# A state-space layer on one core: where the transposed blocks are kept, when they are loaded back, and what stands ahead of the multiply by dt

## The chip, the cores and the metric

The kernel runs on one core of a Trainium2 chip. The metric is the device time of one execution in microseconds (us): 1695.08 us as the median of three runs (1694.08 to 1696.36).

The engines are TensorE (PE in the profile; its weight loads are PEld), VectorE (DVE), ScalarE (ACT), GpSimd (POOL) and SyncE (SP). Here SyncE issues all of the transfers. Each engine works through its own list of instructions in order, and semaphores are what holds one list back for another.

## The reference

Input is `x` of 2 x 512 tokens of width 512. The layer is a Mamba-2 block with a residual, then a dense layer with summed low-rank experts and another residual:

```
proj  = layernorm(x) @ in_proj_w.T             # gate 8192 | x 8192, B 1024, C 1024 | dt 128
hBC   = silu(causal_conv(x, B, C; 4 taps))
dt    = clip(softplus(dt + dt_bias), 0, 100);  A = -exp(A_log)
xch   = hs * dt                                # 128 heads of 64, chunks of 128 tokens
Y     = (C B^T * exp(segsum(dt*A))) @ xch      # inside a chunk
      + C @ (states carried over the chunks)   # states = B^T @ (decay * xch)
      + hs * D
g     = Y * silu(gate);  g = g * rsqrt(mean over each of 8 groups of g^2 + 1e-5)
x     = x + (g * norm_w) @ out_proj_w.T
x     = x + layernorm(x) @ W.T + b + sum_e probs_e (layernorm(x) @ A_e.T) @ B_e.T
```

Everything is fp32. The large products are made of three: weight and input are each split into a high part that TensorE's fp32r form holds and the rest (`w_high`, `w_low`), and high x high, high x low and low x high are added.

## The kernel before

The work is cut into 64 units. A unit k is 128 of the 8192 inner channels, that is two heads, over all 1024 tokens; eight units (j = 0 to 7) are one group g, which shares B and C. Each engine has a hand-written function `body(g, last)`, which goes through the eight j and issues for unit k what is due, and for unit k+1 (`ahead`) what can be done early. Nothing but the order of these calls and the semaphores sets the schedule.

TensorE's body for unit k: the last two output products of the unit before (`later_outs`, c = 2 and 3), the projection of the x channels of unit k+1 into `x_bank` (24 matmuls of 512 columns), `states(k)`, which needs `xdecay`, then `diagonal(k)`, the gate projection of unit k+1 into `g_bank` (24 more), `carry(k)`, and the output products c = 0 and 1. Bodies 4 and 5 of a group also project B and C of the next group, and bodies 6, 7 and 0 have smaller products.

The path of unit k+1 from its convolution to `xdecay` is this. ScalarE's `tap0` writes tap 0 from `x_bank` into `hs`. VectorE's `tap` adds taps 1 to 3 (L1234), ScalarE applies silu (L1079). VectorE's `turn_blocks` (L1317) transposes each 32 x 32 block of `hs`; SyncE's `store_blocks` (L714) stores the result to `blocks_dram` in DRAM (512 KB), and after the store has landed `load_quads` (L721) brings it back with four transfers into `quads` in another arrangement, so that tokens are on the partitions. VectorE's `to_heads` (L1332) multiplies `quads` by dt into `xdt`, in two instructions; GpSimd's `decayed` (L1526) multiplies `xdt` by the decay into `xdecay`, one instruction for each of the two batches b. Only then can TensorE start `states(k+1)` (L823).

Before the change, `turn_blocks(k+1)` writes its result over the `hs` buffer of unit k, so it comes after `skip(k)` (L1296, the last reader of that buffer), and ScalarE's `tap0` waits for the store of the blocks that lie where it writes. SyncE issues, between the store and `load_quads`, the four transfers of `load_grown` (L707), which wait for VectorE's `add_carry` (L1303). On VectorE `to_heads(k)` stands behind the two scores multiplications (L1266) and behind `add_outs` for c = 2 and 3 (L1355, or the copy at L1352 in two of the eight units), which wait for TensorE's `later_outs`. In bodies 5 and 6 it stands behind the three taps of B or C (L1243) as well.

Behind `to_heads(k)` VectorE has `y_low_part` (L1250), in body 1 also the sum of squares and the reciprocal, in bodies 1, 2 and 3 `normed_out` (L1359, two, three and three instructions), and then the taps of unit k+1.

## Time and profile before

| | |
|---|---|
| median of three runs | 1695.08 us |
| the profiled execution: its own time | 1687.36 us |
| its span, first to last instruction | 1685.6 us |
| PE busy | 1570.0 us (93%) |
| DVE busy | 1376.5 us (82%) |
| ACT busy | 1149.9 us (68%) |
| POOL busy | 758.2 us (45%) |
| mean granted TensorE clock | 0.984 |

The span is the time between the first and the last instruction of the profiled execution; its own time is 1.8 us more. Busy times can overlap between engines. The first `states` starts at 69.6 us and the last at 1621.4 us, so the 64 units take some 1552 us of the span; what is before is the first layernorm and the tables, what is after is the last group's norm and the dense layer. In the profile's rows "[1.98 <-POOL xdecay L1526]" means that the engine stood idle for 1.98 us before this instruction and that the instruction named released it.

### The profile page before, as it was taken

What the parts mean: (1) busy time and instruction counts of PE and PEld (TensorE: products, weight loads), DVE (VectorE), ACT (ScalarE), POOL (GpSimd) and SP (SyncE); (2) the same over time, 40 slices, a digit from 0 to 9 for tenths busy, and PEclk for the clock granted to TensorE, in tenths of its full rate; (3) what the DMA queues carried; (4) which work ended last, traced back from release to release, by engine and by line L of the source; (5) the groups of instructions that cost most, each with busy time, mean ns of one, the idle gap of its engine ahead of it and who ended that gap; (6) DMA issues with size and microseconds to landing.
All of it is one profiled execution on the core that took longest, in us unless ns stands there. A gap on an engine that the chain in (4) does not pass through costs nothing.

```text
span 1685.6 us, 26384 instructions
## 1 busy us (share of the span) xinstructions
PE 1570.0 (93%) x9072; PEld 1311.4 (78%) x9072; DVE 1376.5 (82%) x2047; ACT 1149.9 (68%) x2020; POOL 758.2 (45%) x535
## 2 busy tenths in 40 slices
PE   7879999899998999999999999989999899999988
PEld 5667888787887788778887788777788778877767
DVE  7677878887888878887788888788878987888777
ACT  5966667666786677666577667666677767776643
POOL 2244444454445444445345535445444544545440
PEclk9999999999999999999999999999999999999989
DMA  4554434443443344344444344434344334343321
GB/s 150 201 159 129 156 124 134 154 143 108 157 150 127 119 150 149 127 136 129 129 160 138 124 146 136 128 132 156 105 146 160 130 117 158 137 142 126 132 66 51
DMA packets 132278, 228.43 MB, mean 136 GB/s; under 512 B 28080, under 2 KB 76720, under 8 KB 131888
## 3 DMA queue, kind: packets, MB, share of 16 engines
q1 hardware_dynamic: 132144, 226.74, 41.0%
q8 instruction: 73, 1.20, 0.3%
q14 instruction: 61, 0.50, 0.1%
HBM read 187.87 MB, written 38.80 MB: 134 GB/s over the span
## 4 chain that ended last, share of the span: by engine, by line
issue 55%; POOL 36%; PE 7%; ACT 1%; DVE 0%; DMA 0%; SPq 0%; POOLq 0%; ACTq 0%; DVEq 0%
POOL w_low L1505 9%; POOL xdecay L1526 8%; POOL square_sum L1513 8%; POOL y L1519 6%; POOL out_low L1544 5%; PE head_bank L823 0%; PE d_bank L834 0%; DMA alog<-a_log 0%; PE head_bank L298 0%; PE g_bank L814 0%; PE g_bank L884 0%; PE d_bank L903 0%; PE g_bank L816 0%; PE head_bank L903 0%; PE d_bank L904 0%
## 5 line engine op out<-in xcount | busy, mean ns | idle before, releaser
L1526 POOL TENSOR_TENSOR xdecay<-xdt,tables 128x384 f32<-128x384 f32 x128 | 165.7, 1314 | 478.5 <-DVE xdt L1332 468.4
L1054 ACT ACTIVATE scores<-scores,tables 128x128 f32<-128x128 f32 x1024 | 312.0, 389 | 0.0
L1519 POOL TENSOR_TENSOR y<-y,gate 128x512 f32<-128x512 f32 x128 | 179.5, 1423 | 272.0 <-DVE y L1303 272.0
L1234 DVE SCALAR_TENSOR_TENSOR hs<-x_bank,cols,hs 128x1022 f32<-128x1022 f32 x189 | 241.6, 1278 | 29.9 <-ACT hs L1067 25.3
L814 PE MATMUL g_bank<-x_high,w_high 128*128 128x512 f32 x624 | 251.0, 402 | 0.0
L816 PE MATMUL g_bank<-x_high,w_low 128*128 128x512 f32 x624 | 243.4, 390 | 0.0
L815 PE MATMUL g_bank<-x_low,w_high 128*128 128x512 f32 x624 | 243.4, 390 | 0.0
L1505 POOL TENSOR_TENSOR w_low<-raw,w_high 128x512 fp32r<-128x512 f32 x139 | 184.9, 1330 | 102.6 <-ACT w_high L1044 102.5
L1067 ACT ACTIVATE hs<-x_bank,cols 128x1024 f32<-128x1024 f32 x63 | 75.7, 1201 | 215.8 <-PE x_bank L816 186.0
L823 PE MATMUL head_bank<-xdecay,b_tok 128*128 128x128 f32 x768 | 120.4, 308 | 90.8 <-POOL xdecay L1526 83.8
L814 PE MATMUL x_bank<-x_high,w_high 128*128 128x512 f32 x504 | 196.4, 390 | 1.8 <-issue 1.8
L823 PEld LDWEIGHTS head_bank<-xdecay,b_tok 128*128 128x128 f32 x768 | 104.3, 207 | 119.0 <-POOL xdecay L1526 106.9
L815 PE MATMUL x_bank<-x_low,w_high 128*128 128x512 f32 x504 | 196.1, 389 | 0.0
L816 PE MATMUL x_bank<-x_high,w_low 128*128 128x512 f32 x504 | 196.1, 389 | 0.0
L1266 DVE TENSOR_TENSOR scores<-scores,bc 128x1024 f32<-128x1024 f32 x128 | 174.6, 1375 | 1.4 <-ACT scores L1059 1.4
L814 PEld LDWEIGHTS g_bank<-x_high,w_high 128*128 128x128 f32 x624 | 117.0, 188 | 33.5 <-issue 11.0
L1513 POOL TENSOR_TENSOR square_sum<-square_sum,gate 128x1024 f32<-128x1024 f32 x55 | 137.4, 2499 | 0.0
L816 PEld LDWEIGHTS g_bank<-x_high,w_low 128*128 128x128 f32 x624 | 117.1, 188 | 25.4
L815 PEld LDWEIGHTS g_bank<-x_low,w_high 128*128 128x128 f32 x624 | 117.3, 188 | 22.7 <-issue 0.2
L834 PE MATMUL d_bank<-scores,xdt 128*64 128x128 f32 x2048 | 134.8, 288 | 0.0
L1355 DVE TENSOR_TENSOR acc<-d_bank,acc 128x512 f32<-128x512 f32 x94 | 64.6, 687 | 83.0 <-PE d_bank L873 83.0
L1059 ACT ACTIVATE scores<-scores 128x1024 f32<-128x1024 f32 x128 | 128.6, 1053 | 0.7
(213 smaller groups left out, 3457.6 us busy)
## 6 DMA issues: line engine op xcount, KB each, us to landing
scores<-sums_dram SPq DMA_DIRECT2D x128, 512.0 KB, 4.9
raw<-w_in SPq DMA_DIRECT2D x144, 256.0 KB, 2.7
blocks_dram<-hs SPq DMA_DIRECT2D x63, 512.0 KB, 2.6
quads<-blocks_dram SPq DMA_DIRECT2D x252, 128.0 KB, 3.0
grown_rows<-grown_dram SPq DMA_DIRECT2D x256, 96.0 KB, 2.8
out_raw<-w_out SPq DMA_DIRECT2D x64, 256.0 KB, 3.3
mixed<-x SPq DMA_DIRECT2D x8, 256.0 KB, 4.6
out<-mixed SPq DMA_DIRECT2D x8, 256.0 KB, 2.0
```

The source lines that it names most:

```text
L814: pe.matmul(to, w_high[:, slot, k], x_high[:, b, k], start=(k == 0), stop=False)
L815: pe.matmul(to, w_high[:, slot, k], x_low[:, b, k], start=False, stop=False)
L816: mm = pe.matmul(to, w_low[:, slot, k], x_high[:, b, k], start=False, stop=(k == KT - 1))
L823: mm = pe.matmul(head_bank[b][:, c * P:(c + 1) * P], b_tok[:, b, c], xdecay[:, b, c].rearrange("p r d -> p (r d)"), start=True, stop=True)
L834: mm = pe.matmul(d_bank[r * HEAD_DIM:(r + 1) * HEAD_DIM, b, c * P:(c + 1) * P], xdt[:, b, c, r], scores[:, s, b, r, c], start=True, stop=True)
L1054: op = s.activation(at, at, ACT.Relu, bias=col[:, r, c:c + 1], scale=-1.0)
L1234: v.scalar_tensor_tensor(out=hs[:, q % 2, :, i:], in0=x_bank[:, :, 0:SEQ - i], scalar=cols[:, q, TAPS - 1 - i:TAPS - i], in1=hs[:, q % 2, ...
L1266: v.tensor_tensor(at, at, bc[:, b].rearrange("p c l -> p (c l)").unsqueeze(1) .to_broadcast([P, PAIR, SEQ]), ALU.mult).then_inc(scores_rea ...
L1505: pool.tensor_tensor(w_low[:, slot], raw[:, slot], w_high[:, slot].bitcast(F32), ALU.subtract)\
L1513: pool.tensor_tensor(square_sum[:], square_sum[:], gate[:, q % 2], ALU.add).then_inc(square_added, 1)
L1519: pool.tensor_tensor(y[:, b], y[:, b], gate[:, q % 2, b], ALU.mult).then_inc(y_ready, 1)
L1526: pool.tensor_tensor(xdecay[:, b], xdt[:, b, 0:LATER], col.unsqueeze(3).to_broadcast([P, LATER, PAIR, HEAD_DIM]), ALU.mult)\
```

## The change

It has three parts.

1. `turn_blocks(k+1)` writes into `quads`, the buffer that `load_quads` fills later, and no longer into the `hs` buffer of unit k. It therefore no longer waits for `skip(k)` and is called ahead of it; it waits for `to_heads(k)` (`xdt_ready`), the last reader of `quads`, instead. ScalarE's `tap0` no longer waits for the store. `load_quads` drops its own wait for `xdt_ready`.
2. SyncE issues `load_quads` directly behind `store_blocks`, ahead of the four transfers of `load_grown`.
3. On VectorE, the scores and `to_heads(k)` come ahead of `add_outs` for c = 2 and 3, and in bodies 5 and 6 ahead of the taps of B and C.

```diff
--- before.py
+++ after.py
@@ -672,9 +672,7 @@
         def bank_of(j, c):
             return last_bank[c] if j == UNITS + 1 else out_bank[c]
 
-        def blocks_of(k):
-
-            return hs[:, (k - 1) % 2].rearrange("p b n -> p (b n)")
+        blocks = quads[:].rearrange("p a b c i -> p (a b c i)")
 
         def table_of(kind, b, q):
             return tables[:, b, q // HALF, kind, PAIR * (q % HALF):PAIR * (q % HALF + 1)]
@@ -711,11 +709,10 @@
                 sp.wait_ge(blocks_turned, k)
                 for m in range(QUADS):
                     reached(sp, moved[m], 16 * (k - 1))
-                sp.dma_start(blocks_dram, blocks_of(k)).then_inc(blocks_stored, 16)
+                sp.dma_start(blocks_dram, blocks).then_inc(blocks_stored, 16)
 
             def load_quads(k):
                 sp.wait_ge(blocks_stored, 16 * k)
-                sp.wait_ge(xdt_ready, PAIR * k)
                 by_part = blocks_dram.rearrange("(a j) (m n) -> m j a n", a=QUADS, m=QUADS)
                 for m in range(QUADS):
                     sp.dma_start(quads[m * QUAD:(m + 1) * QUAD].rearrange("p a b c i -> p a (b c i)"), by_part[m])\
@@ -775,9 +772,9 @@
                         load_weight(*at)
                     if ahead:
                         store_blocks(ahead[2])
+                        load_quads(ahead[2])
                         for b in range(BATCH):
                             load_grown(ahead[2], b)
-                        load_quads(ahead[2])
                     for at in then if len(splits) == SPLIT else []:
                         load_weight(*at)
                     if last and j == UNITS - 1:
@@ -1063,7 +1060,6 @@
                     s.wait_ge(cols_in[q // HALF], 16 * (g + 1))
                 s.wait_ge(projected, BATCH * (tile_number(g, place(g, q)) + 1))
                 reached(s, skip_added, k - 1)
-                reached(s, blocks_stored, 16 * (k - 1))
                 s.activation(hs[:, q % 2], x_bank[:], ACT.Identity, scale=cols[:, q, TAPS - 1:TAPS],
                              bias=cols[:, q, TAPS:TAPS + 1]).then_inc(tap0_ready, 1)
 
@@ -1313,8 +1309,8 @@
 
             def turn_blocks(k):
                 v.wait_ge(hs_ready, k + 1)
-                v.wait_ge(skip_added, k)
-                v.transpose(blocks_of(k).rearrange("p (m n i) -> p n m i", m=QUADS, i=QUAD),
+                reached(v, xdt_ready, PAIR * k)
+                v.transpose(blocks.rearrange("p (m n i) -> p n m i", m=QUADS, i=QUAD),
                             hs[:, k % 2].rearrange("p b (c m i) -> p (b c) m i", c=CHUNKS, i=QUAD))\
                  .then_inc(blocks_turned, 1)
 
@@ -1417,20 +1413,16 @@
                     if k == 0:
                         for b in range(BATCH):
                             first_heads(b)
-                    if k > 2:
-                        add_outs(g, j - 1, (2,))
+                    if last or j not in (5, 6):
+                        for b in range(BATCH):
+                            score(g, j, k, b)
+                    if k > 0:
+                        to_heads(g, j, k)
                     if j in (5, 6) and not last:
                         for i in range(1, TAPS):
                             bc_tap(i, 2 * (g + 1) + j - 5, j - 5)
-                    scores_here = last or j not in (5, 6)
-                    if scores_here:
-                        score(g, j, k, 0)
                     if k > 2:
-                        add_outs(g, j - 1, (3,))
-                    if scores_here:
-                        score(g, j, k, 1)
-                    if k > 0:
-                        to_heads(g, j, k)
+                        add_outs(g, j - 1, (2, 3))
                     if j == UNITS - 1 and not last:
                         keep_bc(g + 1, g_bank)
                     if prev and ahead:
@@ -1447,8 +1439,8 @@
                     for b in range(BATCH):
                         carried_state(*now, b)
                     if ahead:
+                        turn_blocks(k + 1)
                         skip(j, k)
-                        turn_blocks(k + 1)
                         for b in range(BATCH):
                             carry_part(k, b)
                         for b in range(BATCH):
```

No instruction is added or removed; what moves is their order. The line numbers of the changed kernel are two to four lower. In its rows, L1313 is `turn_blocks`, L1292 `skip`, L1328 `to_heads`, L1262 the scores.

VectorE in a middle unit of a group, from the end of body k to the first part of body k+1, before:

```order
L1296 SCALAR_TENSOR_TENSOR y<-hs,cols,d_bank 128x1024
L1317 STREAM_TRANSPOSE hs<-hs 128x8x4x32
L1291 TENSOR_TENSOR grown_rows<-head_bank,grown_rows 128x384 x2
L1303 TENSOR_TENSOR y<-y,grown_rows 128x384 x2
L1355 TENSOR_TENSOR acc<-x_bank,acc 128x512 x2
L1355 TENSOR_TENSOR acc<-d_bank,acc 128x512
L1266 TENSOR_TENSOR scores<-scores,bc 128x1024
L1355 TENSOR_TENSOR acc<-d_bank,acc 128x512
L1266 TENSOR_TENSOR scores<-scores,bc 128x1024
L1332 TENSOR_TENSOR xdt<-quads,tables 128x8x64 x2
L1250 SCALAR_TENSOR_TENSOR y_low<-y,cols,y_high 128x1024
```

and with the change:

```order
L1313 STREAM_TRANSPOSE quads<-hs 128x8x4x32
L1292 SCALAR_TENSOR_TENSOR y<-hs,cols,d_bank 128x1024
L1287 TENSOR_TENSOR grown_rows<-head_bank,grown_rows 128x384 x2
L1299 TENSOR_TENSOR y<-y,grown_rows 128x384 x2
L1351 TENSOR_TENSOR acc<-x_bank,acc 128x512 x2
L1262 TENSOR_TENSOR scores<-scores,bc 128x1024 x2
L1328 TENSOR_TENSOR xdt<-quads,tables 128x8x64 x2
L1351 TENSOR_TENSOR acc<-d_bank,acc 128x512 x2
L1246 SCALAR_TENSOR_TENSOR y_low<-y,cols,y_high 128x1024
```

The transpose now stands ahead of `skip`, and both additions from `d_bank` stand behind `xdt`.

VectorE at the start of body 5, where the taps of B are, before:

```order
L1355 TENSOR_TENSOR acc<-x_bank,acc 128x512 x2
L1266 TENSOR_TENSOR scores<-scores,bc 128x1024 x2
L1355 TENSOR_TENSOR acc<-d_bank,acc 128x512
L1243 SCALAR_TENSOR_TENSOR bc_conv<-g_bank,tap_bc,bc_conv 128x2x511
L1243 SCALAR_TENSOR_TENSOR bc_conv<-g_bank,tap_bc,bc_conv 128x2x510
L1243 SCALAR_TENSOR_TENSOR bc_conv<-g_bank,tap_bc,bc_conv 128x2x509
L1355 TENSOR_TENSOR acc<-d_bank,acc 128x512
L1332 TENSOR_TENSOR xdt<-quads,tables 128x8x64 x2
L1250 SCALAR_TENSOR_TENSOR y_low<-y,cols,y_high 128x1024
```

and with the change:

```order
L1351 TENSOR_TENSOR acc<-x_bank,acc 128x512 x2
L1262 TENSOR_TENSOR scores<-scores,bc 128x1024 x2
L1328 TENSOR_TENSOR xdt<-quads,tables 128x8x64 x2
L1239 SCALAR_TENSOR_TENSOR bc_conv<-g_bank,tap_bc,bc_conv 128x2x511
L1239 SCALAR_TENSOR_TENSOR bc_conv<-g_bank,tap_bc,bc_conv 128x2x510
L1239 SCALAR_TENSOR_TENSOR bc_conv<-g_bank,tap_bc,bc_conv 128x2x509
L1351 TENSOR_TENSOR acc<-d_bank,acc 128x512 x2
L1246 SCALAR_TENSOR_TENSOR y_low<-y,cols,y_high 128x1024
```

Here `xdt` moves ahead of five instructions, three of which are the taps of B.

SyncE's queue in a middle unit, before:

```order
L700 DMA scores<-sums_dram 128x1024 x2
L692 DMA raw<-w_in 128x512
L714 DMA blocks_dram<-hs 128x1024
L707 DMA grown_rows<-grown_dram 64x384 x4
L721 DMA quads<-blocks_dram 32x4x256 x4
L696 DMA out_raw<-w_out 128x512
```

and with the change:

```order
L698 DMA scores<-sums_dram 128x1024 x2
L690 DMA raw<-w_in 128x512
L712 DMA blocks_dram<-quads 128x1024
L718 DMA quads<-blocks_dram 32x4x256 x4
L705 DMA grown_rows<-grown_dram 64x384 x4
L694 DMA out_raw<-w_out 128x512
```

The four loads of `quads` and the four of `grown_rows` have changed places.

## Rows read from the trace of the kernel before

**Rows 1.** Page part 1: busy us, share of the span, instructions

```profile
PE 1570.0 (93%) x9072; PEld 1311.4 (78%) x9072; DVE 1376.5 (82%) x2047; ACT 1149.9 (68%) x2020; POOL 758.2 (45%) x535
```

**Rows 2.** Waits over the whole span: total us, times, longest us

```profile
PE head_bank L823 <- POOL xdecay L1526: 83.8, 57, 5.1
...
DVE xdt L1332 <- DMA quads<-blocks_dram: 49.8, 32, 3.1
...
PE head_bank L823 <- issue: 6.9, 7, 2.0
```

**Rows 3.** Timeline of TensorE, units 8 to 11: start us, us, instruction, [idle before]

```profile
267.23 1.69 PE L823 MATMUL head_bank<-xdecay,b_tok 128*128 128x128 f32 x12 [0.82 <-issue]
...
289.59 1.73 PE L823 MATMUL head_bank<-xdecay,b_tok 128*128 128x128 f32 x12
291.26 1.97 PE L834 MATMUL d_bank<-scores,xdt 128*64 128x128 f32 x32
...
313.10 0.94 PE L823 MATMUL head_bank<-xdecay,b_tok 128*128 128x128 f32 x6 [1.98 <-POOL xdecay L1526]
...
337.70 0.94 PE L823 MATMUL head_bank<-xdecay,b_tok 128*128 128x128 f32 x6 [2.58 <-POOL xdecay L1526]
338.94 1.11 PE L823 MATMUL head_bank<-xdecay,b_tok 128*128 128x128 f32 x6 [0.31 <-POOL xdecay L1526]
339.99 3.41 PE L834 MATMUL d_bank<-scores,xdt 128*64 128x128 f32 x32
```

**Rows 4.** Timeline of VectorE, body of unit 10, then xdt of unit 11

```profile
316.45 3.90 DVE L1234 SCALAR_TENSOR_TENSOR hs<-x_bank,cols,hs 128x1022 f32<-128x1022 f32 x3
...
322.69 1.27 DVE L1296 SCALAR_TENSOR_TENSOR y<-hs,cols,d_bank 128x1024 f32<-128x1024 f32 x1
324.07 1.25 DVE L1317 STREAM_TRANSPOSE hs<-hs 128x1024 f32<-128x1024 f32 x1
...
334.46 1.29 DVE L1332 TENSOR_TENSOR xdt<-quads,tables 128x512 f32<-128x512 f32 x2 [2.08 <-DMA quads<-blocks_dram]
335.67 1.28 DVE L1250 SCALAR_TENSOR_TENSOR y_low<-y,cols,y_high 128x1024 fp32r<-128x1024 f32 x1
```

**Rows 5.** Timeline of SyncE's DMA issues in the same stretch

```profile
325.35 0.32 SPq L714 DMA_DIRECT2D blocks_dram<-hs  x1
...
329.19 1.95 SPq L721 DMA_DIRECT2D quads<-blocks_dram  x4
```

**Rows 6.** DMA issues: KB each, median us to landing

```profile
blocks_dram<-hs SPq DMA_DIRECT2D x63, 512.0 KB, 2.6
quads<-blocks_dram SPq DMA_DIRECT2D x252, 128.0 KB, 3.0
```

**Rows 7.** Timeline of GpSimd in units 11 and 31

```profile
335.83 3.06 POOL L1526 TENSOR_TENSOR xdecay<-xdt,tables 128x384 f32<-128x384 f32 x2 [6.27 <-DVE xdt L1332]
...
838.89 1.64 POOL L1526 TENSOR_TENSOR xdecay<-xdt,tables 128x384 f32<-128x384 f32 x2 [7.01 <-DVE xdt L1332]
```

**Rows 8.** Line 1359 on VectorE: ns least/median/most, first and last start

```profile
L1359 DVE SCALAR_TENSOR_TENSOR mixed<-acc,g_rstd,mixed x64: 741/1324/1761, 290.6 to 1671.5; 128x512 f32<-128x512 f32 x64
```

**Rows 9.** Windows: busy us by engine, then PEclk; first and last dip

```profile
93.40:117.70 24.30, 19.52 (x108) 15.59 (x108) 17.16 (x26) 15.80 (x28) 10.05 (x8) 0.93 0.56 179
...
1506.40:1531.00 24.60, 23.20 (x128) 19.31 (x128) 21.88 (x32) 15.46 (x29) 12.88 (x10) 0.93 0.38 134
```

**Rows 10.** Timeline of VectorE, SyncE and TensorE, body of unit 12, then unit 13

```profile
376.19 3.36 DVE L1266 TENSOR_TENSOR scores<-scores,bc 128x1024 f32<-128x1024 f32 x2
382.38 0.69 DVE L1355 TENSOR_TENSOR acc<-d_bank,acc 128x512 f32<-128x512 f32 x1 [2.83 <-PE d_bank L873]
...
387.41 1.29 DVE L1332 TENSOR_TENSOR xdt<-quads,tables 128x512 f32<-128x512 f32 x2
...
374.58 0.32 SPq L714 DMA_DIRECT2D blocks_dram<-hs  x1
...
390.64 1.62 PE L823 MATMUL head_bank<-xdecay,b_tok 128*128 128x128 f32 x11 [1.50 <-POOL xdecay L1526]
```

## The prediction, made before the changed kernel ran

> **What bounds the kernel now.** I read the page's first part, then the waits, then the timeline of each engine over some middle units, then windows for the clock. TensorE is busy for 93% of the span [rows 1], so the question is what ends its idle time. The waits answer it: at the first matmul of `states` (L823) it stood idle for 83.8 us over 57 times because `xdecay` was not there, and 6.9 us more at the same line are put down to issue [rows 2]. That is 90.7 us, most of what TensorE is idle at all (1685.6 - 1570.0 = 115.6 us). Wherever the wait is absent the unit simply takes TensorE's own work: unit 9 comes 22.36 us after unit 8 with no idle time before it, while unit 10 takes 23.51 us of which 1.98 is idle, hence 21.5 us of work, and unit 11 takes 24.60 us with 2.58 idle before it [rows 3].
>
> The idle time costs a second time. In unit 11, behind the 2.58 us, the second six matmuls of `states` and `diagonal` take 1.11 and 3.41 us; in the others they take 0.94 (the first six at 337.70) and 1.97 [rows 3]. That is 1.6 us more, and the windows show why: the granted clock of such a unit is 0.93 of full, that is, one stretch at 1.2 instead of 2.4 GHz right after the idle time. There are eleven such stretches in the main loop, the first and the last in [rows 9]; each comes at a unit that waited about 2 us or more.
>
> So the length of the main loop hangs on when `xdecay` of the next unit is ready. For unit 11 the path is, by start times: taps 316.45, `skip` 322.69, transpose 324.07 [rows 4], store 325.35, then four `grown_rows` issues, the `quads` issues from 329.19 [rows 5], `xdt` 334.46 after VectorE had stood idle 2.08 us for the last of them [rows 4], `states` 337.70 [rows 3]. In bodies 5 and 6 the queue on VectorE is the obstacle, not the transfer: it waits 2.83 us for TensorE's output product, does one addition and the taps of B, and gets to `xdt` at 387.41, though the store had been issued at 374.58 [rows 10].
>
> **The transpose ahead of `skip`.** It stands 324.07 - 322.69 = 1.38 us earlier, and so does the store. What is late next in its place: `skip`, by 1.25 us. Its readers are `carry_part` and `add_carry`, which wait for TensorE's `carry` as well, and that comes behind all 24 matmuls of the gate projection. I cost it at nothing; without that cover 1.25 us would go onto `y_sum` and so onto GpSimd's multiply by the gate, not onto the path to `xdecay`. The transpose costs what it does now, 1.25 us: source and shape are the same, and the wait for `xdt_ready` is for an instruction a whole body earlier on the same engine.
>
> **The loads right behind the store.** Today 329.19 - 325.35 = 3.84 us lie between the store and the first load [rows 5]. The store's landing takes a median of 2.6 us [rows 6] after an issue of 0.32; with the semaphore I take 3.15 us. Gain 0.7 us. Bounds: 0 (the landing is what ended it) and 0.9. SyncE now stands in the wait for the landing with `load_grown` behind it; those loads go out 1 to 2 us later than now, but are read only in the next unit's `carry_part`, behind the next taps, states and transpose. From the first load to `xdt` it takes 334.46 - 329.19 = 5.27 us, unchanged. So `xdt` of unit 11 can start at 322.69 + 1.25 + 0.05 + 3.15 + 5.27 = 332.4, which is 2.1 us earlier, if VectorE is there: the scores ended at 334.46 - 2.08 = 332.38 with two additions among them, and those (0.6 us apart, 0.69 each [rows 10]) are now behind. It is.
>
> **Additions behind `xdt`.** Today `y_low` (L1250) follows `xdt` directly [rows 4] and GpSimd's pair of `xdecay` takes 3.06 us; where in unit 31 the product with the mask from a PSUM bank follows instead, the pair takes 1.64 [rows 7]. Now the additions, which also read a bank, follow everywhere but in bodies 5 and 6 (there it is the taps, which read a bank too). The first half of `xdecay` should be ready about 2.2 us after `xdt` starts, against 3.24 (337.70 - 334.46): 1.0 us more. Bounds 0 and 1.0; I take 1.0, since unit 31 does just this. Likewise `normed_out` (L1359) spans 741 to 1761 ns [rows 8]; its slow cases run beside GpSimd's work. It now comes 1.3 us later, when the shorter pair is over, so I put three of them at about 2.0 us, not 4.
>
> The Trainium skill, SBUF — State Buffer, "Who interferes with whom", says a VectorE instruction with two SBUF inputs and a GpSimd instruction that reads SBUF exclude each other for the whole instruction. The trace agrees (3.06 against 1.64, 741 against 1761). By that rule the change also moves the scores, which have two SBUF inputs, further into GpSimd's multiply by the gate, and this speaks against it; the first rival below carries that case.
>
> So for unit 11: 2.1 + 1.0 = 3.1 us earlier, against 2.58 + 0.31 us of idle time. The wait is gone there. Does it stay gone once TensorE moves faster? The ring that closes from `xdt` to the next `xdt` in units with three `normed_out` is 1.2 (`xdt`) + 1.25 (additions) + 1.8 (`y_low`, part of it behind GpSimd) + 2.0 + 6.24 (taps to transpose, 322.69 - 316.45) + 1.3 + 3.15 + 5.27 = 22.2 us, against TensorE's 21.5. It loses 0.7 us a unit for two units, 1.4, and has 3.1 - 1.98 = 1.1 in hand from unit 10. I leave 0.3 us of idle time in seven groups: 2 us.
>
> **Bodies 5 and 6.** `xdt` can start at 374.58 + 3.15 + 5.27 = 383.0 instead of 387.41, 4.4 us earlier against 1.50 us of idle time (the last row of [rows 10]). VectorE then waits for `quads` (it used to wait for the output product). Queued behind: `xdt` itself 1.2, taps of B 3.9 (by the taps of [rows 4]), additions 1.25, `y_low` 1.2, done at about 390.5. TensorE would end the next projection at 390.64 - 1.50 = 389.1, and `tap0` comes behind that, so the next taps start on time or some tenths late. No idle time is left.
>
> **The sum.** Idle time at L823: 90.7, of which I leave 2 us as above and 3 us in the last unit (it has no projection ahead of `states`; its 5.1 us [rows 2] shrink by 2.1): 85.7 gained. Half-clock stretches: 10 of 11 go, 10 x 1.6 = 16. Together 101.7. Against the profiled execution's own time: 1687.36 - 101.7 = 1585.7. The median of the runs is 7.7 us above that execution (1695.08 - 1687.36); I expect the same of the new one and say **1594 us**, with 1582 to 1608 as its own range.
>
> **Rival 1: VectorE becomes the bound in bodies 1 to 4.** In unit 11 it was idle for only 2.08 of 24.60 us, so its work there is 22.5, above TensorE's 21.5. If `normed_out` stays slow and two scores take 3.36 us as at 376.19 [rows 10] rather than 2.4, the work is 23.5, 2.0 too much in two units of each group, less 1.1 in hand: 2.9 us, and a clock stretch of 1.6 with it, times 7 = 31 us. About 1625. For it: the figures are all in the trace. Against: the cause of slow `normed_out` moves away. Chance 0.18.
>
> **Rival 2: other waits of TensorE appear** that are hidden now (the gate's silu, `out_low`, the convolution), and half of the gain goes: 1695 - 51 = 1644. Against: unit 9 runs with no wait. Chance 0.05. Nothing would change if `xdecay` were in truth held by something else than `xdt`, yet GpSimd stands idle for 6.27 us before the pair of unit 11 [rows 7] and starts it right behind `xdt`: 0.02, at 1695.
>
> **Rival 3: slower.** `to_heads` now stands ahead of the additions and of the taps of B and C, so a late `quads` holds up all of VectorE's list, and with it `y_low`, the taps and the next transpose. Each microsecond beyond what is in hand (1.1) is paid in all 63 units. The change is eaten up at 101.7 / 63 + 1.1 = 2.7 us later landing, 5.7 instead of the 3.0 of [rows 6]; at 6.5 us it is 1695 + 50 = 1745. For it: the loads read DRAM that was just written. Against: they do so now, and lose four transfers that stood before them; the longest wait for them was 3.1 us [rows 2]. Chance 0.03.
>
> **Chances and range.** Forecast 0.72, rival 1 0.18, rival 2 0.05, no change 0.02, slower 0.03. A measurement of this kernel can tell 0.2%, 3.4 us. Faster 0.72 + 0.18 + 0.05 = 0.95, same 0.02, slower 0.03. The range runs from 1580 (all eleven clock stretches gone and 0.9 us from the loads) to 1628, which takes in rival 1.
>
> **What would show it.** Right: the wait at `states` below 10 us in all; units 10 to 12 at about 21.5 us and the units of bodies 5 and 6 1.5 us shorter; the first load 3.1 to 3.2 us behind the store; `xdecay` pairs near 1.7 us; a mean clock near 0.99. Wrong: VectorE without idle time in units 10 to 12 while TensorE still waits for `xdecay` (rival 1); a new line among TensorE's waits (rival 2); VectorE's wait for `quads` well above 49.8 us [rows 2] with the landing above 5 us (rival 3).

## The result and the profile after

The changed kernel takes **1591.67 us** in the median of 4 runs (1585.43 to 1595.86), the one before 1695.72 (4 runs, 1694.08 to 1696.83). The ratio is 0.9384 with a 95% interval of 0.9345 to 0.9423. The forecast was 1594, and for the profiled execution 1585.7; that execution took 1585.43.

Page part 1 of the kernel after, which answers to [rows 1]:

```profile
PE 1537.4 (97%) x9072; PEld 1295.0 (82%) x9072; DVE 1395.8 (88%) x2047; ACT 1144.6 (72%) x2020; POOL 737.0 (47%) x535
```

The span is 1583.7 us. TensorE is idle for 1583.7 - 1537.4 = 46.3 us, where it was 115.6: 69.3 less. Its busy time has fallen too, by 32.6 us, with the same 9072 matmuls. Together that is the 101.9 us by which the span is shorter. So the gain has two parts, and the forecast's sum (85.7 of idle time, 16 of clock) has the right total with a different split.

The waits of the kernel after (total us, times, longest us), against [rows 2]:

```profile
DVE xdt L1328 <- DMA quads<-blocks_dram: 73.4, 31, 5.8
...
PE head_bank L838 <- DVE state L1276: 9.8, 15, 2.8
...
PE head_bank L820 <- POOL xdecay L1518: 6.0, 3, 2.9
...
PE d_bank L831 <- DVE acc L1351: 4.8, 6, 1.6
```

Line 820 is `states`, 823 before. Its 90.7 us of idle time are now 6.0. Two new lines appear that the forecast's sum did not have: `carry` (L838) waits for the state, and `diagonal` (L831) waits for an addition to `acc`, 14.6 us together. 84.7 won less 14.6 given back is 70.1, within a microsecond of the 69.3. VectorE's wait for `quads` has grown from 49.8 to 73.4 us. Most of it costs TensorE nothing; where it does is shown below.

Timeline of TensorE after, from the `states` of unit 10 to that of unit 11, which answers to [rows 3]:

```profile
294.78 1.50 PE L820 MATMUL head_bank<-xdecay,b_tok 128*128 128x128 f32 x12
296.21 1.97 PE L831 MATMUL d_bank<-scores,xdt 128*64 128x128 f32 x32
...
303.69 1.50 PE L838 MATMUL head_bank<-c_feat,state 128*128 128x128 f32 x12
```

No row has idle time before it, and the twelve matmuls of `states` take 1.50 us in one piece. The next `states` starts at 315.92, so the unit takes 21.14 us, where 24.60 was and where the forecast's "TensorE's own work" was 21.53. The mean granted clock over the whole span is 0.996 against 0.984; of the eleven half-clock stretches of the main loop one is left.

Timeline of VectorE after, for the same unit, which answers to [rows 4]:

```profile
294.83 2.06 DVE L1355 SCALAR_TENSOR_TENSOR mixed<-acc,g_rstd,mixed 128x512 f32<-128x512 f32 x3
296.81 3.90 DVE L1230 SCALAR_TENSOR_TENSOR hs<-x_bank,cols,hs 128x1022 f32<-128x1022 f32 x3
...
303.06 1.24 DVE L1313 STREAM_TRANSPOSE quads<-hs 128x1024 f32<-128x1024 f32 x1
304.22 1.24 DVE L1292 SCALAR_TENSOR_TENSOR y<-hs,cols,d_bank 128x1024 f32<-128x1024 f32 x1
...
308.57 3.39 DVE L1262 TENSOR_TENSOR scores<-scores,bc 128x1024 f32<-128x1024 f32 x2
311.89 1.28 DVE L1328 TENSOR_TENSOR xdt<-quads,tables 128x512 f32<-128x512 f32 x2
313.09 1.27 DVE L1348 COPY acc<-d_bank 128x512 f32<-128x512 f32 x2
314.29 1.67 DVE L1246 SCALAR_TENSOR_TENSOR y_low<-y,cols,y_high 128x1024 fp32r<-128x1024 f32 x1
```

Three `normed_out` take 2.06 us (forecast 2.0), and `xdt` (311.89) follows the scores with no wait: VectorE's list and the transfer are level here. GpSimd's pair behind it, against [rows 7]:

```profile
313.25 1.64 POOL L1518 TENSOR_TENSOR xdecay<-xdt,tables 128x384 f32<-128x384 f32 x2 [3.50 <-DVE xdt L1328]
```

SyncE's issues in the same unit and the DMA table (KB, median us to landing), against [rows 5, 6]:

```profile
304.32 0.32 SPq L712 DMA_DIRECT2D blocks_dram<-quads  x1
307.32 1.75 SPq L718 DMA_DIRECT2D quads<-blocks_dram  x4
309.11 2.37 SPq L705 DMA_DIRECT2D grown_rows<-grown_dram  x4
...
blocks_dram<-quads SPq DMA_DIRECT2D x63, 512.0 KB, 3.2
quads<-blocks_dram SPq DMA_DIRECT2D x252, 128.0 KB, 2.9
```

From the store to the first load it is 3.00 us (3.84 before), and from the first load to `xdt` 4.57 (5.27 before), which the forecast had held unchanged. The loads themselves are issued in 1.75 instead of 1.95 us.

**Where the new waits come from.** Timelines of SyncE, VectorE and TensorE after, from the store of unit 22's blocks (j = 6) to its `carry`:

```profile
563.69 0.32 SPq L712 DMA_DIRECT2D blocks_dram<-quads  x1
567.56 3.19 SPq L718 DMA_DIRECT2D quads<-blocks_dram  x4
...
573.75 1.29 DVE L1328 TENSOR_TENSOR xdt<-quads,tables 128x512 f32<-128x512 f32 x2 [5.62 <-DMA quads<-blocks_dram]
...
579.98 3.11 DVE L1246 SCALAR_TENSOR_TENSOR y_low<-y,cols,y_high 128x1024 fp32r<-128x1024 f32 x1
...
579.52 1.97 PE L831 MATMUL d_bank<-scores,xdt 128*64 128x128 f32 x32 [1.61 <-DVE acc L1351]
...
588.18 0.94 PE L838 MATMUL head_bank<-c_feat,state 128*128 128x128 f32 x6 [1.00 <-DVE state L1276]
```

Here the store goes out at 563.69 and `xdt` starts 10.06 us later, against 311.89 - 304.32 = 7.57 us in unit 11. VectorE stands idle for 5.62 us with everything queued behind `xdt`: the taps of B or C, the additions, `y_low`, the next taps, the state. So `diagonal` and `carry` are late. Two things add up here. The store goes out late in these bodies, behind a weight load, and in this unit the transfer itself is slower: 3.87 us to the first load and 6.19 from there to `xdt`, with the four loads issued over 3.19 us, where unit 13 (j = 5; store at 350.24, first load at 353.96, `xdt` at 358.55) has 3.72 and 4.59. Why it was slower there is not known. This is the third rival's mechanism, at work in single units.

The unit times by place j in the group of eight, each from the `states` of the unit before to its own, as the median of six units (8 to 55), worked out from the starts of the first `states` matmul in the timelines; the last row is the mean time of a whole group of eight:

```
j       before  only_p2  parts_12  only_p3  after  norm_spread  spread_and_early_store
0        22.91    21.98     21.98    22.95  21.82        21.81                   21.82
1        22.66    22.33     22.34    22.25  22.05        22.05                   22.05
2        23.55    21.78     21.48    25.25  21.13        21.13                   21.13
3        24.59    22.64     21.94    28.62  21.48        21.14                   21.14
4        24.46    22.56     21.97    27.91  22.00        21.19                   21.14
5        28.46    28.46     28.46    26.81  26.58        26.92                   26.58
6        28.48    28.46     28.48    26.58  26.58        26.58                   26.58
7        23.17    23.18     23.18    24.53  24.17        24.18                   22.94
group    198.9    191.7     189.9    205.5  187.3        187.0                   184.9
```

### The profile page after: what moved, and what is told of

It reads as the page before. It is cut to its first block, busy times and chain, and to the rows that moved or that the text cites. A ratio compares the mean times of both kernels' runs of the same rounds, so it can differ in the third digit from the quotient of the medians.

```text
span 1583.7 us, 26305 instructions
## 1 busy us (share of the span) xinstructions
PE 1537.4 (97%) x9072; PEld 1295.0 (82%) x9072; DVE 1395.8 (88%) x2047; ACT 1144.6 (72%) x2020; POOL 737.0 (47%) x535
## 4 chain that ended last, share of the span: by engine, by line
issue 54%; POOL 37%; PE 7%; ACT 1%; DVE 0%; DMA 0%; SPq 0%; POOLq 0%; ACTq 0%; DVEq 0%
POOL square_sum L1505 9%; POOL y L1511 9%; POOL w_low L1497 8%; POOL xdecay L1518 6%; POOL out_low L1536 5%; DMA alog<-a_log 0%; PE head_bank L298 0%; PE g_bank L811 0%; PE d_bank L831 0%; PE g_bank L881 0%; PE d_bank L900 0%; PE head_bank L900 0%; PE d_bank L901 0%; PE g_bank L813 0%; PE head_bank L902 0%
## 5 line engine op out<-in xcount | busy, mean ns | idle before, releaser
L1511 POOL TENSOR_TENSOR y<-y,gate 128x512 f32<-128x512 f32 x128 | 207.4, 1640 | 236.6 <-DVE y L1299 236.6
L1497 POOL TENSOR_TENSOR w_low<-raw,w_high 128x512 fp32r<-128x512 f32 x139 | 188.1, 1353 | 253.1 <-ACT w_high L1041 253.1
L1518 POOL TENSOR_TENSOR xdecay<-xdt,tables 128x384 f32<-128x384 f32 x128 | 107.0, 856 | 283.3 <-DVE xdt L1328 273.2
L1262 DVE TENSOR_TENSOR scores<-scores,bc 128x1024 f32<-128x1024 f32 x128 | 205.4, 1643 | 1.7 <-ACT scores L1056 1.7
L1328 DVE TENSOR_TENSOR xdt<-quads,tables 128x512 f32<-128x512 f32 x126 | 81.3, 686 | 78.2 <-DMA quads<-blocks_dram 73.4
L1505 POOL TENSOR_TENSOR square_sum<-square_sum,gate 128x1024 f32<-128x1024 f32 x55 | 141.5, 2572 | 0.0
L831 PE MATMUL d_bank<-scores,xdt 128*64 128x128 f32 x2048 | 126.0, 276 | 4.8 <-DVE acc L1351 4.8
L1276 DVE SCALAR_TENSOR_TENSOR state<-state,chunk_tab,head_bank 128x64 f32<-128x64 f32 x512 | 121.0, 278 | 9.1
L831 PEld LDWEIGHTS d_bank<-scores,xdt 128*64 128x64 f32 x2048 | 110.5, 137 | 13.0 <-DVE acc L1351 5.9
```

What stands on the lines that cost most here:

```text
L831: mm = pe.matmul(d_bank[r * HEAD_DIM:(r + 1) * HEAD_DIM, b, c * P:(c + 1) * P], xdt[:, b, c, r], scores[:, s, b, r, c], start=True, stop=True)
L1262: v.tensor_tensor(at, at, bc[:, b].rearrange("p c l -> p (c l)").unsqueeze(1) .to_broadcast([P, PAIR, SEQ]), ALU.mult).then_inc(scores_rea ...
L1497: pool.tensor_tensor(w_low[:, slot], raw[:, slot], w_high[:, slot].bitcast(F32), ALU.subtract)\
L1505: pool.tensor_tensor(square_sum[:], square_sum[:], gate[:, q % 2], ALU.add).then_inc(square_added, 1)
L1511: pool.tensor_tensor(y[:, b], y[:, b], gate[:, q % 2, b], ALU.mult).then_inc(y_ready, 1)
L1518: pool.tensor_tensor(xdecay[:, b], xdt[:, b, 0:LATER], col.unsqueeze(3).to_broadcast([P, LATER, PAIR, HEAD_DIM]), ALU.mult)\
```

## The experiments

Each kernel was timed in 3 rounds beside the kernel before on the same chip; that one took 1695.70, 1695.75 and 1693.31 us in the three groups of runs, and each ratio is to its own group. Part 1 is the transpose into `quads` and ahead of `skip`, part 2 the loads right behind the store, part 3 `xdt` ahead of the additions.

**The three parts alone.** The edits are the three parts of the diff that is shown ahead of the prediction, one at a time (part 1 with the waits that change with it, which are left out here).

```
only_p1: -  skip(j, k)                      only_p2: -  load_grown(ahead[2], b)   (four)
         -  turn_blocks(k + 1)  # into hs            -  load_quads(ahead[2])
         +  turn_blocks(k + 1)  # into quads         +  load_quads(ahead[2])
         +  skip(j, k)                               +  load_grown(ahead[2], b)
only_p3: to_heads ahead of add_outs 2 and 3, and of bc_tap in bodies 5 and 6
```

> The kernel before with part 1 alone (blocks turned into quads, transpose ahead of skip). Theory A, the ledger: what counts is when xdecay is ready, unit by unit. The transpose comes 1.4 us earlier, which helps the units where xdt waits for the transfer (j = 2, 3, 4) and not those where VectorE's own list holds it (j = 0, 5, 6). Per group 1.4 + 1.4 + 0.9 us of idle time and one half-clock stretch of 1.6, 5.3 us, times 7: about 1658 us. Theory B: the transfers alone matter, and VectorE's order only in bodies 5 and 6; the same here, about 1658. Idle time at states in bodies 5 and 6 stays 1.5 us each in both.

> The kernel before with part 2 alone (loads right behind the store). Theory A and B: 0.7 us earlier in the units with j = 2, 3, 4, nothing elsewhere, perhaps one half-clock stretch fewer in every second group: 2.1 + 0.8 us a group, about 1675 us. If the landing of the store is what the first load waited for all along, 1695.

> The kernel before with part 3 alone (scores and xdt ahead of the additions and of the taps of B and C). Theory A: besides the 1.5 us in each of bodies 5 and 6, the pair of xdecay no longer meets y_low and is 1.0 us sooner everywhere else, normed_out mostly misses GpSimd, and the half-clock stretches go with the longer waits: per group 3.0 + 0.8 + 3.0 + 1.6 = 8.4 us, about 1633 us, with xdecay at a mean below 1000 ns. Theory B: only bodies 5 and 6, 3.0 us a group, about 1674 us.

Measured: part 1 alone 1687.78 us, 0.9968 (0.9946 to 0.9990). Part 2 alone 1626.12 us, 0.9601 (0.9569 to 0.9633). Part 3 alone 1735.55 us, 1.0246 (1.0201 to 1.0290). All three expectations were missed: the second part carries most of the gain by itself, the first does nearly nothing alone, and the third costs 40 us. The 8 us of part 1 are small beside the spread of its ten runs (1684.31 to 1699.07), and its profiled execution does not show them: a group of eight units takes 199.2 us there, 198.9 before.

Why part 1 does little alone is in VectorE's and SyncE's timelines of `only_p1`, for the loads of unit 11:

```profile
325.77 1.01 DVE L1299 TENSOR_TENSOR y<-y,grown_rows 128x384 f32<-128x384 f32 x2
...
323.79 0.32 SPq L712 DMA_DIRECT2D blocks_dram<-quads  x1
326.35 2.37 SPq L705 DMA_DIRECT2D grown_rows<-grown_dram  x4
328.76 2.01 SPq L718 DMA_DIRECT2D quads<-blocks_dram  x4
```

The store goes out earlier, but the `grown_rows` loads come next on this in-order queue. They follow the store by 2.56 us, in `only_p3` below by 1.37, but the first row, `add_carry`, by 0.58 and 0.57: it is this addition that they wait for, and it has hardly moved (in unit 10 it starts 12.83 us behind `states`, 13.05 before). The `quads` loads stand behind them, 4.97 us after the store. So part 1 is worth little without part 2.

Why part 3 costs is in `only_p3`. Its waits:

```profile
DVE xdt L1332 <- DMA quads<-blocks_dram: 187.9, 59, 5.1
...
PE head_bank L841 <- DVE state L1280: 51.6, 40, 3.8
```

And its timelines of TensorE, VectorE, SyncE and GpSimd over unit 10:

```profile
310.78 1.73 PE L823 MATMUL head_bank<-xdecay,b_tok 128*128 128x128 f32 x12 [1.72 <-POOL xdecay L1522]
...
323.84 0.94 PE L841 MATMUL head_bank<-c_feat,state 128*128 128x128 f32 x6 [2.15 <-DVE state L1280]
...
312.53 6.22 DVE L1359 SCALAR_TENSOR_TENSOR mixed<-acc,g_rstd,mixed 128x512 f32<-128x512 f32 x3
318.67 3.90 DVE L1234 SCALAR_TENSOR_TENSOR hs<-x_bank,cols,hs 128x1022 f32<-128x1022 f32 x3
...
328.37 1.00 DVE L1303 TENSOR_TENSOR y<-y,grown_rows 128x384 f32<-128x384 f32 x2
...
336.86 1.29 DVE L1332 TENSOR_TENSOR xdt<-quads,tables 128x512 f32<-128x512 f32 x2 [2.92 <-DMA quads<-blocks_dram]
...
327.57 0.32 SPq L714 DMA_DIRECT2D blocks_dram<-hs  x1
328.94 2.37 SPq L707 DMA_DIRECT2D grown_rows<-grown_dram  x4
331.41 1.95 SPq L721 DMA_DIRECT2D quads<-blocks_dram  x4
...
311.49 2.25 POOL L1501 TENSOR_TENSOR w_low<-raw,w_high 128x512 fp32r<-128x512 f32 x1
313.69 2.81 POOL L1509 TENSOR_TENSOR square_sum<-square_sum,gate 128x1024 f32<-128x1024 f32 x1
```

In the kernel before, the three `normed_out` of this unit are this row:

```profile
312.27 4.26 DVE L1359 SCALAR_TENSOR_TENSOR mixed<-acc,g_rstd,mixed 128x512 f32<-128x512 f32 x3
```

VectorE's wait at the head of its list (49.8 before, 187.9 us now) makes all behind it late: the three `normed_out` now run beside GpSimd's `w_low`, `square_sum` and what follows them without a gap, and take 6.22 us, where the kernel before has 4.26 and the changed one 2.06, the taps are late, the state is late, `carry` waits for it, and the next transpose and store are late in turn, which closes the ring. The sum is 28.6 us per unit of j = 3 in place of 24.6. `xdecay` is indeed quick behind `xdt`, and it doesn't matter. The Trainium skill, SBUF — State Buffer, "Who interferes with whom", has it that a VectorE instruction with two SBUF inputs contends with a GpSimd instruction that reads SBUF. The 6.22 against 2.06 agrees. The forecast feared it for the scores; it struck at `normed_out`, by lateness.

**Pairs.** The edits are two of the three parts each.

> The changed kernel without part 3. Theory A: 2.1 us earlier in j = 2, 3, 4, which leaves 0.8 us in j = 3, 3.0 us in bodies 5 and 6 and 0.8 in j = 0; half-clock stretches gone: 6.5 us a group gained, about 1647 us. Theory B: all is gained but bodies 5 and 6, about 1615 us.

> The changed kernel without part 2. Theory A: 2.4 us of the 3.1 remain per unit, so the waits at states stay away at first, but the ring from xdt to xdt is 0.7 us longer (22.9 against TensorE's 21.5), and about 1 us comes back in each of two units of a group: about 1604 us. If the order of SyncE's queue is worth nothing, 1592 us. If the landing of quads is what delays single units, it should be neither better nor worse here.

> The changed kernel without part 1 (the transpose stays behind skip and writes the other hs buffer). Theory A: 1.7 us of the 3.1 remain, so about 1 us of idle time a unit is left in j = 3 and 4 and the ring is 1.4 us longer: about 1615 us. Rival: the transpose's place is worth its full 1.4 us in all 63 units: 1680 us.

Measured: `parts_12` 1611.78 us, 0.9512 (0.9485 to 0.9539). `parts_13` 1731.45 us, 1.0208 (1.0187 to 1.0230). `parts_23` 1640.77 us, 0.9669 (0.9643 to 0.9695). Theory B had `parts_12` (1615). The other two were missed: 1604 was expected of `parts_13`, which is 127 us slower than that, and 1615 of `parts_23`.

With the single runs this makes the whole table, in us added by a part to what stands before it:

```
                 on nothing   on one other part              on both others
part 1               -8       -14 (on 2), -4 (on 3)               -49
part 2              -70       -76 (on 1), -95 (on 3)             -140
part 3              +40       +44 (on 1), +15 (on 2)              -20
```

The 4 us of part 1 on part 3 are within the intervals of the two runs; all other steps are clear of them, the 8 us of part 1 alone only just. The parts don't add up, since part 3 changes its sign. It puts VectorE's whole list behind the transfer, which costs as long as the transfer is late (on nothing, on 1, on 2) and pays once parts 1 and 2 together have made it early. The wait of VectorE for `quads` goes 187.9 (3), 189.3 (1 and 3), 103.1 (2 and 3), 73.4 us (all), and TensorE's wait for the state with it: 51.6, 60.2, 32.2, 9.8. In `parts_12` units of one kind are mostly alike to a few hundredths, and the 28.46 of bodies 5 and 6 is still there; that is what part 3 removes.

**Is it the quick `xdecay`?** `y_low_first` is the changed kernel with `y_low` directly behind `xdt` again, as before.

```
+  if prev and ahead: y_low_part(prev[1], prev[2])
   if j in (5, 6) and not last: bc_tap ...
   if k > 2: add_outs(g, j - 1, (2, 3))
-  if prev and ahead: y_low_part(prev[1], prev[2])
```

> The changed kernel with y_low directly behind xdt, the additions and taps behind it. If y_low (two SBUF inputs) is what stretched GpSimd's pair of xdecay, the pair takes about 2.6 to 3.1 us again (mean near 1300 ns instead of 856) and xdecay is ready 1.0 us later: that uses up the slack in j = 2 to 4, idle time of 0.3 to 1 us comes back in two or three units a group, about 1600 us. If the pair was stretched by something else, it stays at 856 ns and the time at 1592.

Measured: 1589.58 us, 0.9375 (0.9354 to 0.9396), so no loss that can be told against the change's 0.9384 (0.9345 to 0.9423). The duration came as expected and the 1600 us did not. The groups of instructions show that the slow pair was back:

```profile
L1518 POOL TENSOR_TENSOR xdecay<-xdt,tables 128x384 f32<-128x384 f32 x128 | 166.6, 1320 | 296.4 <-DVE xdt L1328 286.5 <-DVE xdt L1306 9.9
...
L1246 DVE SCALAR_TENSOR_TENSOR y_low<-y,cols,y_high 128x1024 fp32r<-128x1024 f32 x63 | 80.5, 1278 | 0.0
```

1320 ns each, where the change has 856; and `y_low` 1278, where it has 1606. TensorE waits 11.3 us at `states` (6.0 in the changed kernel), 15.0 at `diagonal` (4.8) and 1.8 at `carry` (9.8), 28.1 instead of 20.6 us in all. The forecast's microsecond per unit from the quicker pair is real as a duration, but the 63 us that it would add up to over the units are not there: the waits of the two profiled executions differ by 7.5 us, and the medians do not tell that from nothing.

**Which half of part 3 pays?** `bc_half_on_12` is parts 1 and 2 with `xdt` moved ahead only in bodies 5 and 6; `bc_half_on_before` has that half alone.

```
   scores_here = last or j not in (5, 6)
+  if not scores_here:
+      to_heads(g, j, k)
+      bc_tap ...
   if k > 2: add_outs(g, j - 1, (2,))
-  if j in (5, 6) and not last: bc_tap ...
   ...
-  if k > 0: to_heads(g, j, k)
+  if k > 0 and scores_here: to_heads(g, j, k)
```

> The kernel before with only that half of part 3 that concerns bodies 5 and 6: xdt ahead of the taps of B and C there, all other bodies as before. Theory C: part 3 made things slower by its other half, in the plain bodies, where xdt waits for quads with the additions and everything behind it held up; in bodies 5 and 6 xdt gains 4 us against 1.5 us of idle time. So 14 x 1.5 = 21 us are gained, about 1675 us. Rival: wherever xdt waits at the head of VectorE's list it costs, bodies 5 and 6 as well: 1700 us or more.

> Parts 1 and 2, and of part 3 only the half in bodies 5 and 6. Theory C: parts 1 and 2 together left 28.5 us periods in bodies 5 and 6, TensorE's own work there is 26.6, and nothing else: 14 x 1.9 = 27 us below 1611.8, about 1585 us, a little below the changed kernel, since the plain half of part 3 is worth nothing. Rival: the plain half carries part of the gain (xdecay's pair at 1.7 us instead of 3.0): 1598 us or more.

Measured: on parts 1 and 2 it takes 1592.99 us, 0.9408 (0.9391 to 0.9425), which can't be told from the whole change; alone 1686.76 us, 0.9959 (0.9938 to 0.9980). So `xdt` ahead of the taps of B and C gives all that part 3 gives in the time of the whole kernel, 19 us. It is less than the 27 expected, since the unit behind (j = 7) goes from 23.18 to 24.16 us: 1.65 + 1.90 - 0.98 = 2.6 us a group, 18 in seven. Its rival (1598 us or more) did not come. The half in the other bodies neither helps nor harms in sum once parts 1 and 2 are in. By the medians of its units the changed kernel is 1.4 us a group ahead of `bc_half_on_12`, and it loses that in single late units (24.99 and 26.41 us in one group); the mean group takes 187.3 us in both.

On the kernel before, that half alone also falls short of its 1675 us. The bodies 5 and 6 take 26.83 and 26.58 us instead of 28.5, but the next two units give half of it back (24.75 and 23.25, against 23.17 and 22.91), and j = 1 to 4 another 0.8 us. That VectorE comes out of bodies 5 and 6 late would explain it; it was not followed through the trace. With this run, the 40 us of part 3 alone are put to its other half, the plain bodies.

**Is it `normed_out` that makes part 3 dear?** `order_only_spread` is part 3 alone with `normed_out` two at a time in four bodies instead of three; `norm_spread` is the same spreading on the whole change.

```
-  {1: (0, 1), 2: (2, 3, 4), 3: (5, 6, 7)}
+  {1: (0, 1), 2: (2, 3), 3: (4, 5)}
+  if j == 4 and g > 0: (6, 7), ahead of the additions, which wait for them
```

> Part 3 alone, which took 1735.6 us, with normed_out spread two a body over bodies 1 to 4. Theory: the 28.3 us periods of j = 3 and 4 are a ring on VectorE and the transfers (xdt, additions, y_low, normed_out, taps, skip, transpose, additions of the carry, grown loads, quads loads), in which normed_out takes 1.7 us each because it comes late enough to meet GpSimd's w_low. One fewer in bodies 2 and 3 shortens the ring by 1.7 us each, and the next ones by less contention: about 1705 us. If the ring is made by the queue's order alone: 1730 us.

> The changed kernel with normed_out spread over bodies 1 to 4, two instructions in each, instead of two, three and three. Theory: what is left above TensorE's own work is VectorE being late in j = 2, 3, 4 (periods of 22 and up to 26 us instead of 21.1), because normed_out runs beside GpSimd when it is late. One fewer in bodies 2 and 3: 0.7 to 1.7 us less there, taps on time, about 1586 us. Rival: late landings of quads cause it, then no change, 1592 us.

Measured: `order_only_spread` 1726.85 us, 1.0192 (1.0170 to 1.0214); `norm_spread` 1582.27 us, 0.9329 (0.9308 to 0.9350). On part 3 alone the units of j = 3 and 4 fall from 28.6 and 27.9 to 26.5 and 26.7, but j = 5 and 7 rise by 1.1 and 1.7: 9 us in all against part 3 alone, with intervals that overlap, where 30 were expected. So the slow `normed_out` is not the cause of that loss. The wait at the head of the list is still there (189.2 us), and is left as the cause; no run took that wait away alone. On the whole change the spreading brings j = 3 and 4 to 21.14 and 21.19 us, and its 1586 us were nearly met. The 9 us between the medians (1591.67 and 1582.27) are more than that explains: the intervals of the ratios just overlap, and the two profiled executions took 1585.43 and 1585.05 us.

**Taking the remaining wait.** `norm_spread` leaves the late loads for the units of j = 5 and 6, whose store SyncE issues in its bodies 4 and 5 behind weight loads. The last kernel puts the store ahead of them there.

```
+  if ahead and j in (4, 5): store_blocks(ahead[2])
   for at in splits[2:]: load_weight(*at)
   ...
-  store_blocks(ahead[2])
+  if j not in (4, 5): store_blocks(ahead[2])
   load_quads(ahead[2])
```

> The changed kernel with normed_out spread over four bodies and, in bodies 4 and 5, the store of the blocks ahead of the weight loads in SyncE's queue (load_quads stays where it is). What is left in norm_spread is units with j = 7 of 24 to 27 us and some of j = 6 of 27.8 instead of 22.9 and 26.6, each behind an xdt of body 6 that came late because the store waited at 13 to 16 us for a weight load. The store then goes out at about 9 us, xdt comes some 3 us earlier, and about 10 us go: 1573 us. Rival: those delays come from slow landings of quads and not from the store: 1582 us.

Measured: **1572.79 us**, 0.9284 (0.9262 to 0.9307), the fastest of all. SyncE's timeline of `norm_spread` in such a body, for unit 21, whose unit time began at 524.63:

```profile
537.31 0.33 SPq L690 DMA_DIRECT2D raw<-w_in  x1
537.82 0.32 SPq L712 DMA_DIRECT2D blocks_dram<-quads  x1
541.86 1.74 SPq L718 DMA_DIRECT2D quads<-blocks_dram  x4
```

and of `spread_and_early_store` (began at 523.02), with a line of TensorE's waits:

```profile
532.66 0.32 SPq L712 DMA_DIRECT2D blocks_dram<-quads  x1
535.39 0.33 SPq L690 DMA_DIRECT2D raw<-w_in  x1
539.30 1.75 SPq L718 DMA_DIRECT2D quads<-blocks_dram  x4
...
PE head_bank L841 <- DVE state L1279: 2.6, 6, 1.3
```

SyncE's waits in `spread_and_early_store` from 532 to 540 us (total us, times, longest us), and the store of this unit in the DMA table (KB, us to landing):

```profile
SPq L718 <- DMA blocks_dram<-quads: 3.6, 1, 3.6
...
blocks_dram<-quads SPq DMA_DIRECT2D x1, 512.0 KB, 6.6
```

Counted from those starts, the store goes out at 9.64 instead of 13.19 us. The loads are issued at 16.28 instead of 17.23 only. What they wait for is the landing of the store, which comes 6.6 us after its issue here and 4.0 in `norm_spread`; it now goes out right behind the two loads of `scores`, 512 KB each, at 531.58. (That these slow it is not tested.) So `xdt` of this unit comes 1.1 us earlier (20.90 against 21.95 us, at 543.92 and 546.58), not 3. The unit of j = 7 falls from 24.18 to 22.94 us. The wait for the state is nearly gone: 2.6 us, 6.2 in `norm_spread` and 9.8 in the changed kernel. The expectation of 1573 us was met and its rival of 1582 us was not, but its step was three times too large in this unit, so that the number came out so near is luck.

## Why the prediction was right

**The bound.** Right. The wait at `states` was what set the length of the main loop, and removing it (90.7 to 6.0 us) gave the gain; the stretches at the lower clock went with it, eleven to one. One reading was off: unit 9 was taken for a unit without a wait, since no idle time stands before its row in [rows 3]. Its weight load had waited:

```profile
289.59 1.54 PEld L823 LDWEIGHTS head_bank<-xdecay,b_tok 128*128 128x128 f32 x12 [0.37 <-POOL xdecay L1526]
```

The weight loads of this line waited 106.9 us for `xdecay`, TensorE's matmuls 83.8, so the latter is too small a count.

**Part 1, 1.38 us earlier.** The transpose does stand ahead of `skip`, but the step costed it apart from part 2, and the runs show that it is worth some 8 us alone and 49 with both others. The step named no queue that the earlier store passes; the `grown_rows` loads behind it on SyncE hold the rest back.

**Part 2, 0.7 us.** Mis-sized. From the store to `xdt` it is 7.57 us in unit 11 after, where it was 3.84 + 5.27 = 9.11: 1.54 us, of which 0.84 lie between store and first load and 0.70 between first load and `xdt`, the interval held unchanged. The 3.15 us of the step also counted the issue of 0.32 us twice, since the landing in [rows 6] is counted from the issue on. The four transfers of `grown_rows` no longer stand ahead of the `quads` there; that their absence is what shortens it was not tested by itself. In `only_p2` the step is even 315.97 - 313.39 = 2.58 us to the first load:

```profile
313.39 0.32 SPq L714 DMA_DIRECT2D blocks_dram<-hs  x1
315.97 1.74 SPq L721 DMA_DIRECT2D quads<-blocks_dram  x4
```

The first interval came within the bounds given (0 to 0.9 us); the sum did not, because the second interval had none.

**Part 3, `xdecay` 1.0 us sooner.** The duration was right (1.64 us a pair, the first half ready about 2.2 us behind `xdt`), its use was wrong: `y_low_first` does without it at no loss that can be told. `normed_out` at 2.0 us was right (2.06 for the three of unit 10), but that is so only while VectorE is on time; in `only_p3` it is 6.22.

**Bodies 5 and 6.** Right: 28.46 and 28.48 became 26.58, and by `bc_half_on_12` this is part 3's whole worth. The step said that the next taps come "on time or some tenths late". In unit 22 `carry` waits 1.00 us behind them, and the cause is in the timeline: `xdt` starts 10.06 us behind the store, not the 8.42 that the step added up (in unit 13 it is 8.31). The unit of j = 7 behind them takes 24.17 us, where it was 23.17.

**The sum.** Two errors of nearly the same size cancelled. The forecast left 14.6 us of new waits out. It also left out what a wait costs besides its idle time: `states` behind a wait takes 1.73 us or 1.69 ([rows 3]), without one 1.50, and a whole unit with no wait takes 21.14 where 23.51 - 1.98 = 21.53 had been computed. Of these 0.39 us some 0.23 are the longer row. The other 0.16 are how the rows are written: matmuls of the projection start 0.23 us apart (294.33, 294.56, then `states` at 294.78) and each is given as 0.39 us long, so that an idle time is counted 0.16 us too short. TensorE's busy time fell by 32.6 us, of which the ten half-clock stretches explain 16 at the forecast's 1.6 us each. Another 2.2 are the last unit, where `states` and `diagonal` ran at a granted clock of 0.50 before (2.93 and 2.96 us) and at full clock after (1.73 and 1.97). The rest, some 14 us, is put to rows of `states` that are shorter without a wait, less those of `carry`, which are longer with one; that split is worked out from single rows and not shown by a run. That the profiled execution came out within a microsecond (1585.43 for 1585.7) is luck and proves nothing of the parts. It was also the fastest of the four; the median stands 6.2 us above it, where 7.7 had been added.

**The rivals.** The first (VectorE as the bound in bodies 1 to 4) came at a fraction of its size: in unit 11 VectorE is busy for 20.89 of 21.14 us and just keeps up, but the units of j = 3 and 4 take 21.48 and 22.00, and 21.14 and 21.19 once `normed_out` is spread. That is 1.2 us a group by the medians, some 8 us in all. The second appeared, at 14.6 us instead of half the gain. The third was given 0.03 as an outcome of the whole change, which holds, but its mechanism is what the case turns on. It was reckoned from a later *landing* of the loads (5.7 us instead of 3.0); their median hardly moved (2.9), that of the store went from 2.6 to 3.2, and single transfers as in unit 22 are slower. What decides in most units is when the store is *issued*, relative to VectorE's list, and the argument against the rival didn't separate part 3 from the parts that make it safe. On the kernel before, part 3 makes it 2.5% slower.

## What to carry to other kernels

Before a DMA-dependent instruction is moved to the head of an in-order engine's list, follow the ring back to itself: what it holds up must not be what issues its own transfer. Make the transfer early first, then move the instruction; in the other order the same edit costs 40 us here instead of giving 20. And on the DMA queue look for what stands between a store and its reload: four loads that wait for something else cost 70 us here, and moving them took no byte away.

## What the runs showed of the hardware

- A wait of TensorE costs more than the idle time that the profile gives: about 0.4 us in a unit's remaining time (21.53 to 21.14, and 28.47 - 1.50 = 26.97 to 26.58 in bodies 5 and 6), though the granted clock of unit 10 before and of unit 11 after is full. Some 0.23 us of it are the first matmuls behind the wait (`states` 1.73 instead of 1.50 us), some 0.16 the way in which ends are recorded.
- A wait that the matmul's row does not show can stand at its weight load: 0.37 us in unit 9, and 106.9 against 83.8 us over the whole kernel before.
- Three `normed_out` instructions take 2.06, 4.26 or 6.22 us, by what GpSimd does beside them; `y_low` takes 1.28, 1.68 or 3.11. An engine that is late meets another neighbour and gets later: such a ring stands at 28.6 us for the unit of j = 3 in `only_p3`, with nothing changed but the order on VectorE.
- A reload of 512 KB just written goes out as soon as the store has landed, where nothing stands between them: 2.58 us behind the store in `only_p2`, 3.00 to 3.87 in the rows of the changed kernel, and 6.64 where two loads of 512 KB had been issued just ahead of the store. It was used 4.6 us after its first issue, 6.2 in the slowest unit shown.
